# A graph-network kernel's filter pass: one-hots of 128 columns, one place in the bank, no clearing product, no places in registers

## The reference

```python
def _L2_gnn_ref(h, e, ..., src, dst):
    hn = linear(h, W_node, b_node)
    ef = ssp(linear(e, W_e1, b_e1))         # ssp(x) = softplus(x) - log 2
    ef = ssp(linear(ef, W_e2, b_e2))
    m = hn[src] * ef                        # one message per edge, 128 wide
    agg = jax.ops.segment_sum(m, dst, num_segments=N)
    out = ssp(linear(agg, W_fc1, b_fc1))
    return linear(out, W_fc2, b_fc2)
...
x = x + _L2_gnn_ref(h, edge_attr_128, ..., src, dst)
```

## Time and profile before

| | us |
|---|---|
| median of 3 executions | 4463.06 |
| lowest, highest | 4462.13, 4468.02 |
| span of the profiled execution | 5773.8 |
| filter pass in it, about | 3278 to 4697 |
| PE busy, share of the span | 3956.3, 69% |
| POOL busy | 2896.8, 50% |
| DVE busy | 2133.2, 37% |
| ACT busy | 1348.1, 23% |
| granted TensorE clock, mean | 0.621 |

### The profile page before, as it was taken

The page is one execution under the profiler, slowest core; times in us unless marked ns, Lnnn a source line. Parts: engine busy times, 40 slices in busy tenths (PEclk is TensorE's granted clock), DMA queues, the critical chain, the costliest instruction groups (busy, mean ns, idle before and its releaser), DMA issues. The chain is left out here.

```text
span 5773.8 us, 76309 instructions
## 1 busy us (share of the span) xinstructions
PE 3956.3 (69%) x20694; PEld 3229.1 (56%) x20695; DVE 2133.2 (37%) x6441; ACT 1348.1 (23%) x1886; POOL 2896.8 (50%) x3007
## 2 busy tenths in 40 slices
PE   3755565567667777777777666676767664888888
PEld 1645555557546666666667544454545442666666
DVE  4932222223544333333345532232323343332332
ACT  1000000000221000010005544444444452332322
POOL 3865655563135555555541255555555536555451
PEclk7555555555665555555557866666666665888888
DMA  4521111110232222222211222222222222111111
GB/s 122 175 57 42 43 42 42 42 43 23 79 132 57 54 58 55 55 58 55 55 49 49 83 75 70 72 79 70 77 72 77 70 70 64 37 35 35 34 36 34
DMA packets 256062, 357.37 MB, mean 62 GB/s; under 512 B 52798, under 2 KB 179189, under 8 KB 255861
## 3 DMA queue, kind: packets, MB, share of 16 engines
q0 software_dynamic: 90624, 185.78, 12.2%
q1 hardware_dynamic: 165241, 169.55, 9.9%
HBM read 316.13 MB, written 39.00 MB: 62 GB/s over the span
## 5 line engine op out<-in xcount | busy, mean ns | idle before, releaser
L797 POOL DMA_INDIRECT m_rows<-table,m_idx x1568 | 1506.9, 961 | 1086.2 <-issue 460.9
L797 POOL DMA_INDIRECT m_rows<-table,e_idx x464 | 444.1, 957 | 373.5 <-DVEq L1347 178.9
L797 POOL DMA_INDIRECT m_more<-table,e_idx x480 | 453.4, 945 | 301.3 <-DVEq L1089 162.3
L1110 PE MATMUL e_agg<-e_weights,m_more 128*128 128x16 f32 x1152 | 339.2, 374 | 308.5 <-DMA lo_dram<-su_lob 176.5
L1110 PEld LDWEIGHTS e_agg<-e_weights,m_more 128*128 128x128 f32 x1152 | 311.7, 330 | 334.2 <-issue 334.2
L1111 PE MATMUL e_agg<-e_weights,m_ones 128*128 128x32 f32 x1568 | 481.6, 401 | 1.7 <-issue 1.7
L1435 PE MATMUL e_out<-e_counts,e_nodes 128*128 128x256 bf16 x2964 | 448.9, 307 | 32.4 <-issue 32.3
L1111 PEld LDWEIGHTS e_agg<-e_weights,m_ones 128*128 128x128 f32 x1568 | 428.3, 333 | 0.9 <-issue 0.9
L1548 PE MATMUL e_z<-e_w,e_filt 128*128 128x128 f32 x1568 | 356.3, 396 | 102.5 <-issue 100.4
L1537 PE MATMUL e_z<-e_edge,e_w 128*128 128x512 f32 x392 | 287.5, 871 | 199.3 <-DVEq L1617 168.8
L1548 PEld LDWEIGHTS e_z<-e_w,e_filt 128*128 128x128 f32 x1568 | 311.3, 293 | 180.6 <-issue 180.3
(11 more groups left out here) (304 smaller groups left out, 6332.4 us busy)
## 6 DMA issues: line engine op xcount, KB each, us to landing
e_edge<-edge_T SPq DMA_DIRECT2D x98, 512.0 KB
lu_place<-lo_dram SPq DMA_DIRECT2D x49, 512.0 KB
m_rows<-table,m_idx POOLq DMA_INDIRECT x1568
e_key<-key_dram SPq DMA_DIRECT2D x98, 256.0 KB
key_dram<-key_out SPq DMA_DIRECT2D x13, 1024.0 KB
table<-m_rows SPq DMA_DIRECT2D x39, 256.0 KB, 2.3
m_more<-table,e_idx POOLq DMA_INDIRECT x480
m_rows<-table,e_idx POOLq DMA_INDIRECT x464
```

The source lines that it names most:

```text
L797: pool.indirect_dma_start(rows[:, t, :], None, table, bass.IndirectOffsetOnAxis(ap=idx[:, t:t + 1], axis=0)).then_inc(landed[q], 16)
L1110: pe.matmul(to[:, 0, cols], s.rows[at.r][:, t, :], both[:, t, 0, :], start=False, stop=False)
```

## The change

`setup_phase` also computes `place_c`, each edge's destination less its *chunk's* first destination: `span[:, 1, :]` (the tile's first destination less the chunk's) times the flag of the narrow path, plus `place_f`. It stores it to DRAM, and the filter pass loads it. The one-hots of the filter pass have 128 columns per tile instead of 16. All 8 tiles are summed in columns 0 to 127 of the bank, the first with `start=True`. The clearing product and the places in registers go.

```diff
--- before.py
+++ after.py
@@ -116,6 +116,7 @@
         span = sb("su_span", [P, 2, T], F32)
         dst_f = sb("su_dst_f", [P, T], F32)
         most = sb("su_most", [P, 4], F32)
+        place_c, placed = sb("su_place_c", [P, T], F32), sem("su_placed")
         loaded = sem("su_loaded")
         lo_ready = sem("su_lo_ready")
         chain = sem("su_chain")
@@ -131,7 +132,9 @@
 
                 sp.wait_ge(lo_ready, 1)
                 sp.dma_start(k.dram["lo_dram"].rearrange("(p t) -> p t", p=P), lo_b[:]).then_inc(stored, 16)
-                sp.wait_ge(stored, 16)
+                sp.wait_ge(placed, 1)
+                sp.dma_start(k.dram["place_dram"], place_c[:]).then_inc(stored, 16)
+                sp.wait_ge(stored, 32)
                 sp.wait_ge(loaded, 80)
 
             @block.gpsimd
@@ -168,7 +171,8 @@
                 ch.add(v.tensor_copy(m.narrow_i[:], most[0:1, 0:1]))
 
                 ch.step(v.tensor_scalar(most[:, 1:2], most[:, 0:1], -1.0, None, ALU.mult))
-                ch.add(v.scalar_tensor_tensor(m.place_f[:], m.base_f[:], most[:, 1:2], dst_f[:], ALU.mult, ALU.add))
+                ch.step(v.scalar_tensor_tensor(m.place_f[:], m.base_f[:], most[:, 1:2], dst_f[:], ALU.mult, ALU.add))
+                v.scalar_tensor_tensor(place_c[:], span[:, 1, :], most[:, 0:1], m.place_f[:], ALU.mult, ALU.add).then_inc(placed, 1)
                 ch.add(v.tensor_copy(m.iota_f[:], m.iota_i[:]))
                 ch.add(v.tensor_copy(m.iota_w[:], m.iota_i[:]))
                 ch.add(v.tensor_copy(m.part_f[:], m.part_i[:]))
@@ -1480,6 +1484,7 @@
         b2_parts, ones_b = sb("b2_parts", [3, G4, P], BF16), sb("ones_b", [3, P], BF16)
         edge, low1, low2, filt1, message = two("edge"), two("low1_"), two("low2_"), two("filt1_"), two("message")
         soft = sb("soft", [P, E], F32)
+        place_c = sb("place_c", [P, k.T], F32)
         neg_b1, shift1 = sb("neg_b1", [P, 1], F32), sb("shift1", [P, 3], F32)
         z1 = ctx.enter_context(nc.psum_tensor("e2_z1", [P, E], F32))
         z2 = [ctx.enter_context(nc.psum_tensor(f"e2_z2_{b}", [P, E], F32)) for b in range(2)]
@@ -1503,7 +1508,7 @@
         with nc.Block() as block:
             @block.sync
             def _(sp):
-                for t, d in ((w1, k.dram["We1T"]), (w2, k.dram["We2T"]), (b1, k.dram["b_e1"].unsqueeze(1)),
+                for t, d in ((place_c, k.dram["place_dram"]), (w1, k.dram["We1T"]), (w2, k.dram["We2T"]), (b1, k.dram["b_e1"].unsqueeze(1)),
                              (b2, k.dram["b_e2"].partition_broadcast(3))):
                     sp.dma_start(t[:], d).then_inc(consts, 16)
 
@@ -1512,7 +1517,7 @@
                     sp.wait_ge(z1_ready, at.n + 1)
                     sp.dma_start(edge[at.b][:], k.dram["edge_T"][:, ds(at.chunk * E, E)]).then_inc(edge_ready[at.b], 16)
                 both_paths(sp, m, lambda wide: over_chunks(sp, k, wide, load))
-                sp.wait_ge(consts, 64)
+                sp.wait_ge(consts, 80)
 
             @block.gpsimd
             def _(pool):
@@ -1520,15 +1525,13 @@
 
             @block.tensor
             def _(pe):
-                pe.wait_ge(consts, 64)
+                pe.wait_ge(consts, 80)
                 pe.wait_ge(shift_ready, 2)
                 pe.matmul(agg[0][0:3, 0:P], shift1[:], w2[:], start=True, stop=True).then_inc(moved_ready, 1)
                 pe.wait_ge(start, SETUP)
                 pe.sem_inc(z1_ready, 2)
 
                 def path(wide):
-                    W = CW if wide else W_NARROW
-
                     def first_product(at):
                         pe.wait_ge(edge_ready[at.b], 16 * (at.pair + 1))
                         pe.wait_ge(z1_free, at.n + 1)
@@ -1549,14 +1552,12 @@
                         ins.then_inc(z2_ready, 1)
 
                     def sums(at):
-                        rel = tile_windows(pe, nc, k, m, at)
                         pe.wait_ge(s.agg_free, at.n + 1)
-                        clear_bank(pe, m, agg[at.b], CW)
                         pe.wait_ge(onehot_ready, at.n + 1)
                         pe.wait_ge(message_ready, at.n + 1)
                         for t in range(C):
-                            ins = pe.matmul(agg[at.b][:, ds(rel[t], W)], message[at.b][:, t * P:(t + 1) * P],
-                                            s.onehot[at.b][:, t * W:(t + 1) * W], start=False, stop=(t == C - 1))
+                            ins = pe.matmul(agg[at.b][:, 0:CW], message[at.b][:, t * P:(t + 1) * P],
+                                            s.onehot[at.b][:, t * CW:(t + 1) * CW], start=(t == 0), stop=(t == C - 1))
                         ins.then_inc(s.agg_ready, 1)
                     walk(pe, wide, [(0, second_product), (2, first_product), (-1, sums)])
                 both_paths(pe, m, path)
@@ -1564,7 +1565,7 @@
             @block.scalar
             def _(act):
                 act.preload_act_table_set("natural_log_exp_and_others")
-                act.wait_ge(consts, 64)
+                act.wait_ge(consts, 80)
 
                 def low_part(at, z, low, bias, chain, ready):
 
@@ -1589,7 +1590,7 @@
             def _(v):
                 for free in s.rows_free:
                     v.sem_inc(free, 1)
-                v.wait_ge(consts, 64)
+                v.wait_ge(consts, 80)
                 reset_windows(v, m, start)
                 ch = Chain(v, start, 1)
 
@@ -1630,7 +1631,11 @@
                         v.sem_inc(s.rows_free[at.r], 1)
 
                     def make(at):
-                        onehot_of(v, m, s, at.chunk, at.w, at.b)[1].then_inc(onehot_ready, 1)
+                        nodes = (m.iota_f if at.w is None else m.iota_w)[:]
+                        where = place_c[:, ds(at.chunk * C, C)]
+                        v.tensor_tensor(s.onehot[at.b][:].rearrange("p (t w) -> p t w", w=CW),
+                                        nodes.unsqueeze(1).to_broadcast([P, C, CW]), over(where, [P, C, CW]),
+                                        ALU.is_equal).then_inc(onehot_ready, 1)
 
                     def add(at):
                         window = acc[:, ds(chunk_window(v, k, m, at), CW)]
@@ -2703,7 +2708,7 @@
     k.dram = {name: nc.dram_tensor(name, value.shape, mybir.dt.from_np(value.dtype), kind="ExternalInput").ap()
               for name, value in arrays.items()}
     k.dram["out"] = nc.dram_tensor("out", (NP, P), F32, kind="ExternalOutput").ap()
-    scratch = {"x_dram": ((NP, P), F32), "line_dram": ((3, NP), F32), "key_dram": ((P, HEADS, NP), F32), "as_dram": ((NP,), F32),
+    scratch = {"x_dram": ((NP, P), F32), "line_dram": ((3, NP), F32), "place_dram": ((P, T), F32), "key_dram": ((P, HEADS, NP), F32), "as_dram": ((NP,), F32),
                "el_dram": ((3, EP), F32), "lo_dram": ((EP,), BF16)}
     for name, (shape, dt) in scratch.items():
         k.dram[name] = nc.dram_tensor(name, shape, dt).ap()
```

## The result

| | median, us | lowest, highest | executions |
|---|---|---|---|
| before, timed beside the change | 4464.39 | 4462.13, 4468.02 | 4 |
| the change | 4512.72 | 4509.31, 4518.76 | 4 |

A forecast was written before the change was run, and what follows sets the result against it. The prediction took GpSimd's gathers to bound the filter pass. Blocked gathers, 49 us, and setup, 4.5, the other terms 0, made +53.5 on 4463.06: 4516 us, range 4425 to 4565, with chances slower 0.60, faster 0.22, same 0.18.

The forecast's parts named there:

- Gathering sets the pace, 8 x 1.25 = 10.0 us per chunk: Filter pass: GpSimd's eight gathers per chunk, 1.25 us apart, set its length; TensorE has 1 us to spare per chunk.
- The late announcements: Filter pass: ACT's second Abs starting some 13 us after its product, every second chunk, comes from recording and is absent unrecorded.
- TensorE: 0: Filter pass: sums with 128 columns add 0.06 to 0.18 us per chunk, the dropped clearing product pays; about 0.
- TensorE bounds, clock rises: Rival: TensorE bounds the filter pass and wide sums keep its clock up, so faster, 4380 to 4430 us; chance 0.22.
- The one-hot: 1.22 us, by itself 0: VectorE, filter pass: the one-hot grows from 0.29 to 1.22 us, +0.93 per chunk, behind the gathers, costing 0 by itself.
- Blocked gathers, +49 us: Filter pass: once more per chunk a gather waits for the one-hot, its operands both in SBUF; 0.5 us, bounds 0 and +107.
- Setup, +4.5 us: End of setup: `place_c`'s operation, 1.03 us, then an uncovered store of 392 KB; +4.5 us, bounds +3 and +9.
- The load ahead of the weights, 0: Start of the filter pass: loading 392 KB before the weights delays no gathers; 0, at worst 3.5 us.
- Absorbed: Rival: the block falls between gathers or into existing waits, so only setup remains, 4467.6 us; chance 0.18.
- VectorE enters the loop: Rival: the one-hot's extra 0.93 us per chunk delays the filter chain, +96, 4559 us; shares 0.60 with blocked gathers.

The follow-up runs named there:

- experiment 7: Before with `soft` written and read by the message in PSUM: 4423.57 us, 0.9904; the change with that and the one-hot's numbers in PSUM: 4436.29 us, 0.9933.
- second look: Before, unedited, recorded once more to stand beside the changed kernel's recording: 4463.64 us in one execution, span 4461.8.
- experiment 3: Before with only the one-hot widened to 128 columns, the sums reading the first 16, no new table: 4518.62 us, ratio 1.0111.
- experiment 4: The change with the one-hot's compared numbers kept in PSUM, in unused columns of the sum banks: 4472.62 us, ratio 1.0008.
- experiment 2: Before with only the new table's setup operation, store and load added, nothing reading it: 4472.87 us, ratio 1.0004.
- experiment 5: Before with `soft` in PSUM, and the change with `soft` and the one-hot's numbers in PSUM: 5815.2 and 5815.99 us, where before took 5801.83.
- experiment 8: The one-hot made twice, in the change and in the change with the one-hot's numbers in PSUM: 5559.27 us (0.9797) and 5680.23 (1.0001).

## Why the prediction was right

Forecast 4516 us, measured 4512.72, by the mechanism named; as a difference, +53.5 forecast and +48.3 measured against the before of the result. By its steps:

- **Gathering sets the pace, 8 x 1.25 = 10.0 us per chunk.** Right, though 10.0 is a little low: 10.33 were left once the message's block was gone, since GpSimd also waits for landings (51.0 us of the pass in experiment 7). The pass took 10.75 us per chunk in its middle in before and 11.26 in the changed kernel. GpSimd waits for no buffer, and the message waits for its rows.
- **The late announcements "I take for the recording".** Wrong. The second look recorded the same kernel, and its span of 4461.8 us has no hold; in two jobs every execution of before took 5.65 to 5.84 ms, profiled or not. What held ACT belongs to the conditions under which that profile was taken. The step came out right for the sum, because the timed executions have no holds either; its reason was wrong, and with it the remark that a profile of the change would show them.
- **TensorE: 0.** Right. From the first start to the last end, the sums of a chunk take 2.45 us in the mean in the changed kernel and 2.46 in before; at the high clock 1.95 and 1.96. Without the clearing product and at the higher clock TensorE does less in all, and none of it reaches the length. The doubt was kept as a rival (TensorE bounds, clock rises). The clock did rise, 0.74 to 0.80. The forecast's reason against the rival, that gathers are the pace, is what experiments 3 and 7 show. The rival's condition fell too: the 0.30 us between gathers stands in recordings as long as the timed executions, so it doesn't belong to the recording. The Trainium skill ("TensorE: Matmul & The Clock Gate", Part 1) says that activity releases the clock; the trace agrees, 0.80 to 0.83 with sums of 128 columns for 0.73 to 0.75 with 16. Here it is worth nothing, because TensorE isn't the pace.
- **The one-hot: 1.22 us, by itself 0.** Right within a few us: 1225 ns, and in PSUM it cost 0.0008 of the time (interval -0.0005 to +0.0022), setup included. The recorded filter passes with it are 9.2 and 5.4 us longer than their counterparts (experiments 4 and 7), some 0.05 to 0.1 us per chunk.
- **Blocked gathers, +49 us.** Right, the term that decides: 54.9 us of excess, 46.4 in the pass's length, that is 0.56 and 0.47 us per chunk for 0.5. The two estimates were 0.48 if the phases were even and 0.6 if they locked. 96 one-hots of 98 caught a gather, and the one shown caught it 0.52 us in: they locked. So the excess was nearer the locked estimate than the 0.5 taken, and what made up for it wasn't in the sum: the idle time between gathers fell from 273.0 us to 265.9, its waits for landings from 58.9 to 43.8. That 49 came within 3 us of 46.4 is in part luck.
- **Setup, +4.5 us.** The mis-sized term: 3.0 in the changed kernel and in experiment 2 (2.6 there counted from the execution's start). The store took 2.7 us from its issue to the next transfer and landed in 2.3. Scaling by size gave 3.5 and was wrong: 392 KB landed in the same 2.3 us as 256.
- **The load ahead of the weights, 0.** Not refuted, and not shown: experiment 2 leaves room for the 3.5 us of its worst case.
- **The rivals.** "Absorbed" fell with 46.4 us; "VectorE enters the loop" fell with experiment 4, where VectorE has all the same work and nearly all of the loss is gone. Sum by the parts: 46.4 + 3.0 = 49.4 us, against 48.3 by the medians and 45.7 between the two recorded spans.

The Trainium skill ("SBUF — State Buffer", section "Who interferes with whom") gives the rule for the blocks: a VectorE instruction with two SBUF inputs and a GpSimd one that reads SBUF contend. By that rule, the trace agrees on both sides: 0.571 us per gather in the mean with two operands in SBUF, 0.1 us in all with one in PSUM. The step from there to this kernel, that an indirect DMA issue counts as a GpSimd instruction that reads SBUF, is not on the page. That section even reports that a `tensor_tensor` was not seen to stall a DMA; here the measurement decides otherwise, for the one-hot is a `tensor_tensor` and 93 of 96 gathers waited for it. The prediction also took from the section that the later one blocks. The runs show that for the gather alone: 97 of the changed kernel's 98 one-hots start while a gather is under way, and they last 1.224 to 1.227 us like the one that doesn't.

## What to carry to other kernels

Before you price a VectorE operation by its own length, ask which memory its operands are in and what GpSimd issues meanwhile: here 0.93 us of extra VectorE time per chunk cost under 10 us in 98 chunks, and half a microsecond of one blocked gather per chunk cost 1%. If gathers set the pace, try to move one operand of each long VectorE operation to PSUM where there is room; for the message in before that alone brought 1% (ratio 0.9904, interval 0.9889 to 0.9919). And compare a profile's span with the timed runs before reading its waits: where they differ by more than a quarter, as 5773.8 and 4463.06 us do, its largest wait may be one that the timed executions don't have.

## What the runs showed of the hardware that was not expected

- **One kernel, two times.** Before took 4454 to 4483 us in jobs one and three but for a single execution of 4689.77, and 5650 to 5835 us in jobs two and four, in every execution. In the latter ACT is held for finished products (684.4 us in the filter pass of experiment 5), and the granted clock in the pass of that kernel is 0.66, for 0.75 in job three:

```profile
3281.40:4723.40 1442.00, 965.89 (x3824) 680.95 (x3824) 429.80 (x507) 614.25 (x589) 745.62 (x809) 0.66 0.23 71
```

  Jobs one and two ran on the same chip, so it is no fixed property of one chip. What it is stays open; the holds are there in every kernel recorded in jobs two and four.
- **More work, less time.** Under the second condition the change with its one-hot doubled, all in SBUF, took 0.9818 (0.9773 to 0.9864) and 0.9797 (0.9745 to 0.9849) of before. With one operand in PSUM it took 1.0023 and 1.0001. The filter pass in experiment 8, doubled in SBUF and then doubled in PSUM:

```profile
3242.60:4514.90 1272.30, 821.02 (x3726) 559.40 (x3726) 638.86 (x605) 616.35 (x589) 822.63 (x809) 0.75 0.29 81
3237.70:4659.90 1422.20, 878.29 (x3726) 601.22 (x3726) 643.90 (x607) 615.25 (x589) 757.33 (x809) 0.71 0.26 73
```

  So the first is 150 us shorter, though its gathers lose 3.5 + 46.4 us in the one-hots and the other's none. ACT stands still for over 8 us 33 times in the first and 45 times in the second. That slower gathering loosens what holds ACT is a guess; it wasn't tried.
- **A block is charged to the gather alone.** The VectorE operation keeps its 1.22 to 1.23 us whether a gather starts in it or is under way when it starts; all the loss is the gather's. Nor does a gather lose if the message starts just behind it: in the changed kernel such gathers, 0.04 to 0.10 us under way, take 0.94 us. And the 16-column one-hot, 0.29 us long with both operands in SBUF, blocked almost nothing: 1.1 us for 49 gathers in three passes.
- **Taking the message's block away brought more than the block.** The gathers' excess was 32.5 us, the pass fell by 37.5, and the time by 42 (0.9904 of 4465.6 us). Of the pass's 37.5 us, 4.9 are idle time between gathers (268.1 us for 273.0). The recorded spans differ by 37.7, all of it in this pass; the other 4 us of the medians are not placed.
